# A two-layer transformer kernel: the last two batches' tails in other slots and other PSUM banks

## The reference

```python
x = x + L0_attn(layernorm(x))   # RoPE, causal, two softmaxes, gate, Wo
x = x + L0_ffn(layernorm(x))    # relu(x W1 + b1) W2 + b2, 512 hidden
x = x + L1_attn(layernorm(x))   # g, b, biases; softmax(q k^T / sqrt(8)) v, no mask
x = x + L1_ffn(layernorm(x))    # (silu(x Wg) * (x Wu)) Wd, 384 hidden, int weights / 127
```

## Time and profile before

| | us |
|---|---|
| median of 3 runs | 354.55 |
| lowest and highest run | 352.91, 355.52 |
| the profiled execution, whole | 355.51 |
| its span | 353.8 |
| mean granted TensorE clock, as a share of 2.4 GHz | 0.942 |

### The profile page before, as it was taken

One profiled execution on the slowest core, in us unless ns is written; L12 is line 12 of the kernel. 1 busy time (PEld: TensorE's weight loads), 2 busy tenths in 40 slices (PEclk: granted clock), 3 DMA queues, 4 the chain that ended last, 5 costly groups with the idle time before them and its releaser, 6 DMA issues.

```text
span 353.8 us, 8365 instructions
## 1 busy us (share of the span) xinstructions
PE 302.2 (85%) x2832; PEld 216.8 (61%) x2832; DVE 252.3 (71%) x993; ACT 223.8 (63%) x501; POOL 168.1 (48%) x383
## 2 busy tenths in 40 slices
PE   1862778597998999999999999999999999998654
PEld 1651556374675767676768676676776666665333
DVE  5776668878677777777776767679798989864422
ACT  6354266867566676767676767597777677768310
POOL 6253347756548486868685625424041403133020
PEclk9986668999899999999999999999999999999966
DMA  7667222312311112323101020020202111000000
GB/s 205 218 152 182 82 63 61 107 45 60 94 46 48 49 47 75 92 77 89 33 2 32 0 56 23 24 55 25 67 25 70 25 38 44 21 15 2 17 15 15
DMA packets 23034, 21.19 MB, mean 60 GB/s; under 512 B 2896, under 2 KB 20048, under 8 KB 22992
## 3 DMA queue, kind: packets, MB, share of 16 engines
q1 hardware_dynamic: 22992, 20.66, 21.1%
HBM read 13.18 MB, written 7.34 MB: 58 GB/s over the span
## 4 chain that ended last, share of the span: by engine, by line
PE 67%; POOL 11%; DVE 9%; ACT 7%; issue 5%; ACTq 0%; POOLq 0%
PE bank L909 14%; PE bank L883 7%; PE bank L939 5%; PE bank L830 5%; PE bank L952 4%; PE bank L866 4%; PE bank L980 4%; PE bank L988 4%; PE bank L887 4%; PE bank L867 4%; POOL RS L394 3%; PE bank L816 3%; POOL XN L401 3%; PE bank L864 2%; ACT PB L546 2%
## 5 line engine op out<-in xcount | busy, mean ns | idle before, releaser
L546 ACT ACTIVATE PB<-bank 128x384 f32<-128x384 f32 (+1 forms) x256 | 134.1, 544 | 54.7 <-PE bank L885 31.0
L711 DVE TENSOR_REDUCE NM<-bank 128x2 f32<-128x512 f32 x128 | 83.7, 683 | 25.2 <-PE bank L867 24.9
L883 PE MATMUL bank<-QS,KS 128*128 128x256 f16 x256 | 70.8, 277 | 6.0 <-ACT PB L546 5.1
L909 PE MATMUL bank<-PB,VP 128*32 128x256 f32 (+1 forms) x1024 | 61.7, 358 | 1.9 <-POOL PB L433 1.2
L706 DVE CUSTOM_DVE_ANT_0 JUNK<-bank,MSF 128x128 bf16<-128x128 f32 x128 | 36.4, 284 | 33.7 <-PE bank L864 33.6
L708 DVE CUSTOM_DVE_ANT_0 JUNK<-bank,MSF 128x256 bf16<-128x256 f32 x128 | 53.7, 420 | 0.0
L909 PEld LDWEIGHTS bank<-PB,VP 128*32 128x32 f32 x1024 | 26.7, 109 | 24.9 <-issue 10.1
L433 POOL TENSOR_SCALAR_AFFINE_SELECT PB<-PB 128x512 f32<-128x512 f32 x64 | 40.7, 636 | 0.0
L460 POOL TENSOR_TENSOR xs<-xs,Y 128x256 f32<-128x256 f32 x8 | 5.8, 727 | 66.2 <-DVE Y L720 66.2
L864 PE MATMUL bank<-KS,QS 96*128 96x256 f16 x128 | 36.1, 287 | 0.0
L883 PEld LDWEIGHTS bank<-QS,KS 128*128 128x128 f16 x256 | 24.8, 97 | 17.7 <-ACT PB L546 15.9
(11 more groups left out here) (90 smaller groups left out, 609.4 us busy)
## 6 DMA issues: line engine op xcount, KB each, us to landing
scr<-PR SPq DMA_DIRECT2D x16, 256.0 KB, 2.9
QS<-scr SPq DMA_DIRECT2D x16, 128.0 KB, 2.7
QS<-scr SPq DMA_DIRECT2D x32, 64.0 KB, 2.9
KS<-scr SPq DMA_DIRECT2D x32, 64.0 KB, 2.9
KS<-scr SPq DMA_DIRECT2D x16, 128.0 KB, 3.2
scr<-PR SPq DMA_DIRECT2D x16, 128.0 KB, 1.9
out_x<-xs SPq DMA_DIRECT2D x8, 128.0 KB, 1.8
W<-in_w SPq DMA_DIRECT2D x1, 576.0 KB, 6.0
```

What stands on the lines that cost most here:

```text
L546: act.activation(PB[:, s % RING, 0:n], TB_[s % 2][:, 0:n], ACT.Exp).then_inc(s_e, 1)
L711: dve.tensor_reduce(m[:, s, 0:2], o[:, :].rearrange("q (n k) -> q n k", n=2), AX.X, ALU.max, negate=True).then_inc(s_mx, 1)
L883: pe.matmul(o[:, 0:S], k[:, 0:P], q[:, :], start=True, stop=True)
L909: ins = pe.matmul(o, v, pr, start=(g % 2 == 0 and kt == 0), stop=True, skip_group_check=True)
```

## The change

For layer 1, batches 6 and 7 (`B - 2`, `B - 1`), steps get slots and banks of their own. In phase 15 the shifted scores go over banks 3, 4, 0 and 1 in turn and wait for the exponential of four slots before. In slots 2 and 3, the first to use banks 0 and 1, they wait for the last maximum instead. In both batches the residual add moves from GpSimd to VectorE (`res_v`), GpSimd keeps only the sum and the power (`rstd3`), and the product of the normalisation is done by VectorE (`normalise3`). Each product of a tail has its bank: for batch 7, the output in 7, the transposes in 3, the gate/up pieces in 0, 1 and 4, Wdown in 5. The steps `hi3` and `th0` to `th2` have names of their own now, in the slots of before for the other batches. For all batches of layer 1, Wdown runs over the three hidden parts outside and the two halves of the rows inside, and waits for each part as it comes to it.

```diff
-        {"bv": (0, 10), ..., "xT3": (1, 13),
-         "lo3": (1, 14), "gu0": (2, 2), "hidden0": (2, 3), "gu1": (2, 5), ...
+        {"bv": (0, 10), ..., "xT3": (1, 13), "hi3": (1, 13),
+         "lo3": (1, 14), "gu0": (2, 2), "th0": (2, 2), "hidden0": (2, 3), ...
-STEP_LAST0 = {...}
+STEP_OF = {(0, B - 1): {...},
+           (1, B - 2): {"oT1": (1, 4), "norm_o": (1, 4), "res": None, "res_v": (1, 4), "bn3": (1, 5), "norm3": None,
+                        "rstd3": (1, 5), "norm3_v": (1, 7), "xT3": (1, 12), "hi3": (1, 11), "lo3": (1, 11), "gu0": (1, 15),
+                        "gu1": (1, 15), "gu2": (1, 15), "th0": (1, 13), "th1": (1, 14), "th2": (1, 15), "hidden0": (1, 15),
+                        "hidden1": (1, 15), "hidden2": (1, 15), "dn": (2, 5), "add_dn": (2, 8)},
+           (1, B - 1): {"oT1": (1, 4), "norm_o": (1, 4), "res": None, "res_v": (1, 5), "bn3": (1, 6), "norm3": None,
+                        "rstd3": (1, 6), "norm3_v": (1, 7), "xT3": (1, 9), "hi3": (1, 9), "lo3": (1, 10), "gu0": (1, 11),
+                        "gu1": (1, 11), "gu2": (1, 11), "th0": (1, 12), "th1": (1, 12), "th2": (1, 12), "hidden0": (1, 13),
+                        "hidden1": (1, 13), "hidden2": (1, 13), "dn": (1, 14), "add_dn": (1, 15)}}
+BANK_OF = {(1, B - 2): {"oT1": 6, "xT3": 2, "gu0": 7, "gu1": 2, "gu2": 6, "dn": 2},
+           (1, B - 1): {"oT1": 7, "xT3": 3, "gu0": 0, "gu1": 1, "gu2": 4, "dn": 5}}
+LAST_T = (3, 4, 0, 1)
...
-    place, count = {}, [0] * 8
-    for _, k, name in sorted(uses):
+    place, count, ahead = {}, [0] * 8, [0] * 8
+    for at, k, name in sorted(uses):
         count[k] += 1
         place[name] = (k, count[k])
-    return place, count
+        if at < H:
+            ahead[k] = count[k]
+    return place, ahead
...
+                    for b in due(1, "rstd3", i, s):
+                        rstd(3, b)
...
+            def scored(i, s):
+                return bank[LAST_T[s % 4]] if i == NPH - 1 else TB_[s % 2]
...
-                act.activation(PB[:, s % RING, 0:n], TB_[s % 2][:, 0:n], ACT.Exp).then_inc(s_e, 1)
+                act.activation(PB[:, s % RING, 0:n], scored(i, s)[:, 0:n], ACT.Exp).then_inc(s_e, 1)
...
+            def normalise3(b):
+                p = b % 2
+                dve.wait_ge(s_rstd[3], 3 * b + 3)
+                for t in range(TPB):
+                    ins = dve.tensor_scalar(XN[3][p][:, t], xs[:, b * TPB + t], MV[:, 3, p, t, 0:1], RS[:, 3, p, t:t + 1],
+                                            ALU.subtract, ALU.mult)
+                ins.then_inc(s_xn[3], 1)
...
+                    for b in due(1, "res_v", i, s):
+                        dve.wait_ge(s_bv, b + 1)
+                        dve.wait_ge(*emptied("oT1", b))
+                        dve.tensor_tensor(xt_(b), xt_(b), halves(Y), ALU.add).then_inc(s_res, 1)
...
+                    for b in due(1, "norm3_v", i, s):
+                        normalise3(b)
...
-                if g >= 2:
+                o = TB_[s % 2]
+                if i == NPH - 1:
+                    o = bank[LAST_T[s % 4]]
+                    if s in (2, 3):
+                        pe.wait_ge(s_mx, H * NPH)
+                    else:
+                        pe.wait_ge(s_e, g - 1 if s < 2 else g - 3)
+                elif g >= 2:
                     pe.wait_ge(s_e, g - 1)
...
             def ffn1_in(c, j):
                 if j == 0:
                     pe.wait_ge(*emptied("xT3", c))
+                if c >= B - 2:
+                    pe.wait_ge(s_mx, H * NPH)
+                if c == B - 1:
+                    pe.wait_ge(s_e, H * NPH)
...
             def ffn1_out(c):
-                pe.wait_ge(*emptied("gu2", c))
                 m = into("dn", c)
-                for t in range(TPB):
-                    for n in range(NG):
+                for n in range(NG):
+                    pe.wait_ge(*emptied(f"gu{n}", c))
+                    for t in range(TPB):
                         ins = pe.matmul(m[:, t * D:(t + 1) * D], HG[:, n, t * P:(t + 1) * P], WD[:, n],
-                                        start=(n == 0), stop=(n == NG - 1))
+                                        start=(t == 0 and n == 0), stop=(n == NG - 1), skip_group_check=True)
```

More of the change, by code:

```diff
@@ L44 @@
          "hi1": (4, 1), "lo1": (4, 10), "v1": (4, 0)},
[2 rows of a table removed]
[3 rows of a table added]
          "dn": (2, 13), "add_dn": (2, 14)})
-STEP_LAST0 = {"xT2": (3, 7), "copy_xT2": (3, 8), "q1": (4, 7), "qk1": (4, 7), "copy_q1": (4, 8), "copy_k1": (4, 8), "hi1": (4, 13), "lo1": (4, 14)}
+STEP_OF = {(0, B - 1): {"xT2": (3, 7), "copy_xT2": (3, 8), "q1": (4, 7), "qk1": (4, 7), "copy_q1": (4, 8), "copy_k1": (4, 8),
+                        "hi1": (4, 13), "lo1": (4, 14)},
+           (1, B - 2): {"oT1": (1, 4), "norm_o": (1, 4), "res": None, "res_v": (1, 4), "bn3": (1, 5), "norm3": None,
[3 rows of a table added]
+           (1, B - 1): {"oT1": (1, 4), "norm_o": (1, 4), "res": None, "res_v": (1, 5), "bn3": (1, 6), "norm3": None,
[3 rows of a table added]
 BANK = {"oT0": 6, "wo": 7, "xT1": 7, "h0": 7, "h1": 7, "f": 6, "xT2": 6, "qk1": 6,
         "oT1": 6, "xT3": 7, "gu0": 7, "gu1": 7, "gu2": 7, "dn": 6}
+BANK_OF = {(1, B - 2): {"oT1": 6, "xT3": 2, "gu0": 7, "gu1": 2, "gu2": 6, "dn": 2},
+           (1, B - 1): {"oT1": 7, "xT3": 3, "gu0": 0, "gu1": 1, "gu2": 4, "dn": 5}}
+LAST_T = (3, 4, 0, 1)
 STAGE_A = {4: dict(bn=-16, norm=-16, xT=-15, q=-13, k=-13, v=-10, rot_q=-12, rot_k=-11, sq_q=-11, sq_k=-10, hi=-9, lo=-7),
@@ L76, in slot_of @@
 def slot_of(L, name, b):
-    off, s = STEP_LAST0[name] if (L, b) == (0, B - 1) and name in STEP_LAST0 else STEP[L][name]
-    return H * (when(L, b) + off) + s
+    at = STEP_OF.get((L, b), {}).get(name, STEP[L].get(name)) if L is not None else None
+    return None if at is None else H * (when(L, b) + at[0]) + at[1]
 def due(L, name, i, s):
@@ L113, in bank_uses @@
         L, b = ORDER[i]
-        uses += [(slot_of(L, name, b), BANK[name], (name, b)) for name in BANK if name in STEP[L]]
-    place, count = {}, [0] * 8
-    for _, k, name in sorted(uses):
+        uses += [(slot_of(L, name, b), BANK_OF.get((L, b), BANK)[name], (name, b)) for name in BANK if name in STEP[L]]
+    place, count, ahead = {}, [0] * 8, [0] * 8
+    for at, k, name in sorted(uses):
         count[k] += 1
         place[name] = (k, count[k])
-    return place, count
+        if at < H:
+            ahead[k] = count[k]
+    return place, ahead
 def head_of_slot(s):
@@ L604, in _ @@
                         act.copy(PR1[b % 2][:, :, 0], QR1[b % 2][:, :, :]).then_inc(s_hi1, 1)
-                    for b in due(1, "xT3", i, s):
+                    for b in due(1, "hi3", i, s):
                         act.wait_ge(*filled("xT3", b))
@@ L608, in _ @@
                     for j in range(NG):
-                        for b in due(1, f"gu{j}", i, s):
+                        for b in due(1, f"th{j}", i, s):
                             act.wait_ge(*filled(f"gu{j}", b))
@@ L879, in shifted @@
                     pe.wait_ge(s_mi[s // HC], 16 * (i + 1))
-                if g >= 2:
+                o = TB_[s % 2]
[6 more added lines that the diff above has]
+                elif g >= 2:
                     pe.wait_ge(s_e, g - 1)
-                q, k, o = QS[L][b % 2][:, s], KS[L][b % 2][:, s], TB_[s % 2]
+                q, k = QS[L][b % 2][:, s], KS[L][b % 2][:, s]
                 pe.matmul(o[:, 0:S], k[:, 0:P], q[:, :], start=True, stop=True)
```

## The result

The changed kernel took 345.36 us (median; 344.94 to 346.76) against 353.73 us (352.80 to 355.52) for the kernel before on the same chip: a ratio of 0.9764, 95% interval 0.9733 to 0.9795, so 2.4% faster. The forecast was 347.1 with 344.8 to 350.2: right in sign, 1.7 us too high. The profiled execution took 346.76, with a span of 345.0.

A forecast was written before the change was run, and what follows sets the result against it. TensorE's order of work was taken to bound most of the kernel, then a single-file chain of engines from phase 15 on. 353.8 + 0.65 - 2.95 - 5.2 = 346.3 span; 7.5 off the median: 347.1 us, range 344.8 to 350.2.

The forecast's parts named there:

- Phase 15: Up to the last group of products of probabilities and V: it starts at 330.95 instead of 330.29, losing 0.65 us.
- 323.35 + 0.60 + 0.4: VectorE in phase 15: batch 6's normalisation, 0.60 us from 323.35, then batch 5's hidden2, done at 325.3.
- Turning to piece 0: Batch 7, from turning its attention output to its first gate/up piece: 6.1 us instead of 9.06, a gain of 2.95.
- the near ends of both bounds: VectorE in batch 7's tail: residual add 0.42 us (at most 0.79), normalisation 0.60 us (other end 1.41).
- T + 4.60: Batch 7's tail: VectorE's normalisation ends 4.60 us after T, the start of turning the attention output.
- Piece 0 to the last add: Batch 7, first gate/up piece to last add: 5.4 us instead of 10.62, gain 5.2; 4.66 at full clock, 5.97 at half.
- The sum: Whole kernel: 0.65 us lost, 2.95 and 5.2 gained, so 7.5 off the 354.55 median, giving 347.1.
- A: Batch 7's tail: TensorE's clock stays full or is back by the second gate/up piece; 346.0 us, chance 0.14.
- B: Phase 15 lengthens by more than 0.65 us, VectorE's statistics and normalisation ahead of batch 5's hidden parts; 348.2 to 350.4, chance 0.12.
- C: TensorE's clock falls in phase 15 itself, costing up to 9 us more; 356, chance 0.03.
- D: Batch 7's gate/up pieces start no earlier because a bank's semaphore is late; tail of old length, 355, chance 0.03.

The follow-up runs named there:

- last_piece_later: Changed kernel with batch 6's three tanh behind exponential 15 and its third gate/up piece behind the last product group: 345.93 us, 0.9759 of the kernel before.
- gpsimd_again: Changed kernel with the residual add and normalisation product of batches 6 and 7 back on GpSimd: 347.13 us, 0.9796 of the kernel before.
- one_bank_pieces: Changed kernel with batch 7's three gate/up pieces all in bank 0 instead of 0, 1 and 4: 349.61 us, 0.9861 of the kernel before.
- wdown_whole: Changed kernel with Wdown as before, waiting for all three hidden parts, rows outside: 348.35 us, 0.9828 of the kernel before.
- keep_clock: Changed kernel with 24 extra matmuls, results unread, behind batch 6's Wdown: 345.64 us, 0.9744 of the kernel before.

## Why the prediction was right

Step by step, in the order of its sum.

- **Phase 15: 0.65 lost; measured 0.59.** The order holds step by step. With the 1.06 us at the mark added, batch 6's first piece started at 328.55 (forecast 328.6), exponential 15 at 330.21 (330.3), the last group at 330.88 (330.95). ScalarE's stall was 1.85 us, forecast 1.5 to 2. The experiments split the result: the banks alone gain 1.04 (14.84 to 13.80), the tanh cost 0.91 (14.51 to 15.42), and what else moved into the phase costs the 0.71 between 13.80 and 14.51. One of batch 6's three pieces ahead of the last group is 0.45 of that (last_piece_later); the rest is not split. One price inside was wrong: batch 6's normalisation took 1.00 and not 0.60, beside GpSimd's add of 0.73 (at 322.32), which I had left out of GpSimd's queue. That this did no harm is luck: the sum "323.35 + 0.60 + 0.4" holds 0.4 us for which it gives no source, just the size of the miss. So the hidden part ended at 325.24 on that scale (forecast 325.3), 0.43 us before Wdown of batch 5 began.
- **Turning to piece 0: 2.95 gained; measured 2.95.** The add took 0.42 and the product 0.60, the near ends of both bounds, with GpSimd idle beside them. Two small misses cancel: the normalised rows came 0.09 later than the T + 4.60 of the sum, and from the transpose's end to piece 0 it took 0.92 instead of 1.0. Of the gain, gpsimd_again gives VectorE's two operations 0.60 where the clock is left out. The rest goes with batch 6's pieces and Wdown no longer standing ahead: the transpose now waits 2.75 us for its rows and for nothing else. No run takes that part alone.
- **Piece 0 to the last add: 5.2 gained; measured 5.33.** The sum lay between 4.66 (full clock) and 5.97 (half); the clock came back within Wdown, at 5.29. In that profile TensorE worked without a pause from 337.49 and had its clock back 2.8 us later; with pauses (one_bank_pieces, wdown_whole) it stayed at half. This agrees with the Trainium skill ("TensorE: Matmul & The Clock Gate", "What's actually happening"), by which the throttled state is the default and activity releases it. But the moment wasn't forecast by more than a guess: in last_piece_later and gpsimd_again, without a pause as well, the clock came back only 4.8 and 5.1 us behind piece 0. The experiments split the gain: the banks 3.62 and the order of Wdown 2.38, each taken away alone, 0.67 more than the 5.33 of both. The clock stayed down in either, and the sum's half-clock figure lies 0.68 above what was measured (5.97 less 5.29); that this is the reason is my reading, not shown.
- **The sum: 7.5; measured 7.74** from the mark to the end of the span (38.35 less 30.61), the store 0.05 of it. Of the 1.7 us by which 347.1 was too high, 0.82 is the median it was taken from, 354.55 of three runs, where the four runs of the result have 353.73. The other 0.9 is the gain, 8.4 us between the medians. Of this the stretches show 0.24. The rest isn't settled; one profiled execution need not be a typical one. In the one used here batch 6's Wdown still ran partly at full clock; in the second profile of the same kernel the tail was 39.45, and from there the gain is 8.8.
- **Rivals.** A (full clock) did not come about; keep_clock shows it 0.55 below what did, and the 0.26 that A takes from the transpose isn't there, since the transpose took 0.44 in both. B did not: the last group was 0.06 early. C did not: the clock was 1.00 in phase 15 in every profile. D did not: no piece of batch 7 waited for a bank.

## What to carry to other kernels

Where a loop of many stages ends, no other work hides the waits of the last rounds. Give each product there a bank of its own, and let each engine's queue hold first what the longest chain wants. What a bank more gains can be lost again to an instruction queued in front of the one that it frees (0.91 of 1.04 us here); ask of every moved step what stands behind it on its engine. Where a tail alternates between engines, count TensorE's work at both clocks: the same three pieces took 1.48 us here at one and 2.74 at the other.

## What the runs showed that I had not expected

The program alone does not fix the moment at which TensorE's clock changes. Two executions of the kernel before differ by 1.15 us in one stretch of its tail and by 1.2 us in the opposite direction between 55 and 63 us, and two of the changed kernel by 1.4 us near 90 us. That is more than the 0.55 us that keep_clock saves in its tail, and more than the 0.45 that last_piece_later gains up to the last group; neither can be seen in the medians.

And VectorE's normalisation took 1.00 us in phase 15, where GpSimd's add began beside it, and 0.60 in the tail, where GpSimd was idle. VectorE's and GpSimd's timelines of the changed kernel:

```profile
322.39 1.00 DVE L687 TENSOR_SCALAR XN<-xs,MV,RS 128x128 f32<-128x128 f32 x2 [0.48 <-POOL RS L411]
322.32 0.73 POOL L491 TENSOR_TENSOR xs<-xs,SM 128x256 f32<-128x256 f32 x1
```

The Trainium skill ("SBUF — State Buffer", "Who interferes with whom") says that a VectorE instruction in a two-port mode and a GpSimd instruction exclude each other, the second waiting for the whole of the first. The trace agrees in direction: 0.40 us were added, though GpSimd's add had 0.66 left to run when VectorE began, so a full block is not shown. The 0.40 is the price to try first where such a pair of operations is moved beside GpSimd's.
